# Window attention: inverse roots of two tiles at once on VectorE, and a new order of the rounds

## What is computed

```
for each of 6 blocks:                       # x is 16 x 256 x 128, 16 heads of 64
    q, k, v = split(x' @ Wqkv)              # x' : half of the channels shifted by one step
    q, k = l2norm(q) * qs, l2norm(k) * ks   # t / max(|t|, 1e-12)
    q, k = rotary(q, cos, sin, scale), rotary(k, cos, sin, 1 / scale)
    attn = softmax(mask(q @ k^T * 8))       # windows of 32 see themselves and the one before
    x = x + (attn @ v) @ Wo
    y = layernorm(shift(x)) * g + b
    x = x + (y1 * gelu(y2)) @ W2 + b2       # y1, y2 = split(y @ W1 + b1), 341 wide each
out = layernorm(x + x_before_the_stack)
```

## Time and profile before

| | us |
|---|---|
| median of 3 executions | 4148.47 (4144.48 to 4149.37) |
| profiled execution, its own time | 4148.09 |
| its span | 4146.3 |
| TensorE busy | 3788.5 (91% of the span) |
| GpSimd busy | 2942.9 (71%) |
| VectorE busy | 2900.7 (70%) |
| ScalarE busy | 2376.3 (57%) |
| mean granted TensorE clock | 0.961 of full speed |

### The profile page before, as it was taken

The page is one execution under the profiler, slowest core; times in us unless marked ns, Lnnn a source line. Parts: engine busy times, 40 slices in busy tenths (PEclk is TensorE's granted clock), DMA queues, the critical chain, the costliest instruction groups (busy, mean ns, idle before and its releaser), DMA issues.

```text
span 4146.3 us, 150150 instructions
## 1 busy us (share of the span) xinstructions
PE 3788.5 (91%) x64432; PEld 2730.8 (66%) x64432; DVE 2900.7 (70%) x5136; ACT 2376.3 (57%) x4221; POOL 2942.9 (71%) x4274
## 2 busy tenths in 40 slices
PE   6888899769999899998999989999899998999997
PEld 3444444357777677776777767777677776777774
DVE  3566655556777777777777777777777777777772
ACT  3322221146667667676666667776667766676662
POOL 0222222378888788887888878888788887888772
PEclk9999999879999999999999999999999999999998
DMA  1000000011111111111111111111111111111110
GB/s 67 3 6 6 6 3 3 16 47 39 38 36 41 46 45 41 38 39 41 48 42 37 40 39 49 42 38 40 40 44 46 39 37 44 42 48 41 40 36 25
DMA packets 96279, 147.03 MB, mean 35 GB/s; under 512 B 27264, under 2 KB 35840, under 8 KB 95488
## 3 DMA queue, kind: packets, MB, share of 16 engines
q1 hardware_dynamic: 95616, 137.42, 13.3%
HBM read 32.46 MB, written 4.19 MB: 9 GB/s over the span
## 4 chain that ended last, share of the span: by engine, by line
PE 80%; DVE 5%; POOL 5%; issue 4%; ACT 4%; DMA 1%; SPq 0%; POOLq 0%; ACTq 0%; DVEq 0%
PE bank L445 18%; PE bank L528 8%; PE bank L517 8%; PE bank L490 6%; PE bank L378 5%; PE bank L465 5%; PE bank L455 4%; PE bank L501 4%; PE bank L585 3%; PE bank L575 3%; PE bank L567 3%; PE bank L393 2%; PE bank L477 1%; POOL m L1341 1%; PE bank L420 1%
## 5 line engine op out<-in xcount | busy, mean ns | idle before, releaser
L445 PE MATMUL bank<-wqkv,xs 128*128 128x512 f32 x3456 | 1123.0, 441 | 18.2 <-DVE m L834 15.7
L1341 POOL TENSOR_TENSOR m<-m 128x512 f32<-128x512 f32 x768 | 969.2, 1283 | 67.8 <-DVE m L834 67.8
L445 PEld LDWEIGHTS bank<-wqkv,xs 128*128 128x128 f32 x3456 | 598.9, 194 | 161.7 <-issue 79.4
L832 DVE TENSOR_TENSOR m<-bank,tab 128x512 f32<-128x512 f32 x768 | 522.0, 680 | 216.3 <-ACT sq L1106 190.3
L1106 ACT ACTIVATE sq<-bank 128x512 f32<-128x512 f32 x768 | 456.4, 594 | 161.3 <-DVE ss L844 78.8
L834 DVE TENSOR_TENSOR m<-bank,tab 128x512 f32<-128x512 f32 x768 | 523.3, 681 | 18.5 <-POOL m L1341 18.5
L844 DVE TENSOR_REDUCE ss<-sq 128x8 f32<-128x512 f32 x768 | 503.4, 677 | 5.9 <-ACT sq L1106 5.1
L1349 POOL TENSOR_TENSOR S<-S,nw 128x1024 f32<-128x1024 f32 x192 | 365.3, 1902 | 193.2 <-DVE S L864 193.1
L517 PEld LDWEIGHTS bank<-P,big 64*64 64x64 f32 x24576 | 376.1, 135 | 97.7 <-issue 96.9
L1357 POOL TENSOR_TENSOR S<-S,rs 128x512 f32<-128x512 f32 x384 | 393.1, 1045 | 23.5 <-DVE rs L878 23.5
L1335 POOL TENSOR_TENSOR m<-m,nw 128x512 f32<-128x512 f32 x384 | 395.4, 1051 | 11.4
(11 more groups left out here) (202 smaller groups left out, 6600.7 us busy)
## 6 DMA issues: line engine op xcount, KB each, us to landing
big<-vst SPq DMA_DIRECT2D x1536, 64.0 KB, 2.0
stage<-in_wqkv SPq DMA_DIRECT2D x36, 256.0 KB, 3.0
tab<-in_tab SPq DMA_DIRECT2D x48, 128.0 KB, 2.3
big<-in_wa SPq DMA_DIRECT2D x1, 3460.0 KB, 12.5
wo<-in_wo SPq DMA_DIRECT2D x6, 512.0 KB, 3.7
big<-in_x SPq DMA_DIRECT2D x8, 256.0 KB, 3.2
keep<-Xr SPq DMA_DIRECT2D x8, 256.0 KB, 2.0
stage<-keep SPq DMA_DIRECT2D x8, 256.0 KB, 3.0
```

Source lines behind the costliest of these rows:

```text
L445: m = eng.matmul(pb[:, :], xt[a], wqkv[:, z, 512 * part:512 * part + 512], start=(n == 0), stop=(n == 2))
L832: eng.tensor_tensor(m1[:, part, :].rearrange("p (h d) -> p h d", d=DH), pv, ct.unsqueeze(1).to_broadcast([P, 8, DH]), ALU.mult)
L1341: eng.tensor_tensor(m1[:, part, :], m1[:, part, :], m2[:, part % 2, :], ALU.add).then_inc(s["g_add"], 1)
```

## The change

The chain moves from POOL to DVE. It is made once for two tiles, in the rounds with odd n, on 72 columns (32 of the even tile, 32 of the odd one, 8 for the layer norms), in nine instructions instead of twelve. The constant factor that two of the dropped instructions applied, `ROOT`, goes into the table of q and into `normed` and `ended`, which multiply by it in the same instruction as before.

Since the roots of an even tile are now ready a round later, all that follows k's scaling runs one tile later: `turn_k`, `mask`, `sim`, `largest`, `lessened`, `weighed` from n-1 to n-2, `exps`, `divide` to n-3, `probs`, `values` to n-4, `out_proj` to n-5; and the once-a-unit steps one unit later. A second buffer, `mk1`, holds parts 2 and 3 of odd tiles; `turned(g, part)` picks it. The loop bodies of PE, DVE, ACT and POOL are laid out anew. The core of the diff:

```diff
-STEPS, ROUNDS = 12, NG + 20
+STEPS, ROUNDS = 9, NG + 20
-ROOT = 1.0
+ROOT = 0.375 * FIRST
-    return STEPS * (g + 1 if g < NG else NG + (g - NG) // 4 + 1)
+    return STEPS * (g // 2 + 1 if g < NG else NG // 2 + (g - NG) // 4 + 1)
+        def turned(g, part):
+            return m1[:, part, :] if part < 2 or g % 2 == 0 else mk1[:, part - 2, :]
@@ vector @@
+            def chain(g):
+                if not 0 <= g < ROUNDS or g % 2 == 0 or g >= NG and g % 4 == 1:
+                    return
+                a = slice(0 if g < NG else 64, 72)
+                nm, y, t = (nw[:, g // 2 % 2, n, a] for n in range(3))
+                if g < NG:
+                    dv.wait_ge("v_ss", 4 * g + 4)
+                    dv.wait_ge("g_scl", 2 * (g - 3))
+                    dv.wait_ge("g_sub", g - 3)
...
+                dv.wait_ge("v_ch", n)
+                eng.tensor_scalar(nm, ss[:, g // 2 % 2, a], 3e38, 1e-24, ALU.min, ALU.max).then_inc(s["v_ch"], 1)
+                dv.wait_ge("v_ch", n + 1)
+                eng.tensor_scalar(y.bitcast(I32), nm.bitcast(I32), -0.5, MAGIC2, ALU.mult, ALU.add).then_inc(s["v_ch"], 1)
+                dv.wait_ge("v_ch", n + 2)
+                eng.tensor_tensor(t, y, y, ALU.mult).then_inc(s["v_ch"], 1)
+                dv.wait_ge("v_ch", n + 3)
+                eng.scalar_tensor_tensor(t, t, -1.0, nm, ALU.mult, ALU.mult).then_inc(s["v_ch"], 1)
...
-                eng.tensor_tensor(xn[:, :], lc, bank[RING["spread"]][:, :], ALU.mult).then_inc(s["v_xn"], 1)
+                eng.scalar_tensor_tensor(xn[:, :], lc, ROOT, bank[RING["spread"]][:, :], ALU.mult, ALU.mult).then_inc(s["v_xn"], 1)
...
-                largest(n - 1)
-                lessened(n - 1)
-                reduced(n, 2)
+                largest(n - 2)
+                if q4 == 3:
+                    norm_step(u - 2)
+                    end_step(u - 5)
                 reduced(n, 3)
...
+                lessened(n - 2)
+                if q4 == 0:
+                    low(u + 1)
+                chain(n)
+                residual(n - 4)
@@ gpsimd @@
-            def chain(g):
...
+                add(n - 1, 3)
+                scale(n - 2, 0)
+                scale(n - 2, 1)
                 add(n, 0)
                 add(n, 1)
...
+                weighed(n - 2)
```

More of the change, by code:

```diff
@@ L247, in _ @@
             eng.dma_start(w2, w2_d[0]).then_inc(s["d_down"], 16)
-            for n in range(NG + 28):
+            for n in range(NG + 32):
                 u, i = n // 4, n % 4
@@ L939, in end_step @@
                 dv.wait_ge("p_ev", k + 1)
-                dv.wait_ge("g_ch", rooted(4 * u + 16))
-                eng.tensor_scalar(ss[:, 0, 36:40], bank[RING["variance"]][:, 0:4], 1e-5, None, ALU.add).then_inc(s["v_e"], 1)
+                dv.wait_ge("v_ch", rooted(4 * u + 19))
+                eng.tensor_scalar(ss[:, 1, 68:72], bank[RING["variance"]][:, 0:4], 1e-5, None, ALU.add).then_inc(s["v_e"], 1)
             def ended(u):
@@ L977, in _ @@
                 weights(n, 3)
+                reduced(n, 2)
                 rotate(n, 3)
@@ L1228, in _ @@
                 q4, u = n % 4, n // 4
+                square(n, 0)
+                weights(n, 0)
+                probs(n - 4, 1)
+                square(n, 1)
+                weights(n, 1)
+                exps(n - 3)
+                if q4 == 1:
+                    gelu(u - 4, 0)
                 if q4 == 0:
                     high(u + 1)
-                probs(n - 3, 1)
-                square(n, 0)
-                weights(n, 0)
                 if q4 == 3:
-                    shifted(u - 1)
-                exps(n - 2)
+                    scaled(u - 3)
+                    shifted(u - 2)
                 if q4 == 1:
-                    gelu(u - 3, 0)
-                if q4 == 3:
-                    scaled(u - 2)
-                if q4 == 1:
-                    gelu(u - 3, 1)
-                square(n, 1)
-                weights(n, 1)
-                out_turned(n - 3, 0)
-                if q4 == 1:
-                    gelu(u - 3, 2)
+                    gelu(u - 4, 1)
                 v_out(n, 0)
                 square(n, 2)
-                turned_k(n - 1, 0)
-                turned_k(n - 1, 1)
+                turned_k(n - 2, 0)
+                turned_k(n - 2, 1)
                 square(n, 3)
-                turned_q(n, 0)
+                if q4 == 3:
+                    centred(u - 2)
+                    end_centred(u - 5)
+                out_turned(n - 4, 0)
+                if q4 == 1:
+                    gelu(u - 4, 2)
+                out_turned(n - 4, 1)
                 v_out(n, 1)
@@ L1258, in _ @@
                 weights(n, 5)
-                out_turned(n - 3, 1)
+                turned_q(n, 0)
                 turned_q(n, 1)
-                if q4 == 3:
-                    centred(u - 1)
-                    end_centred(u - 4)
-                probs(n - 2, 0)
+                probs(n - 3, 0)
         @block.gpsimd
```

223 lines of the change are left out of this document (95 added, 128 removed).

## The result

The changed kernel takes 4155.6 us (median of 19 runs, 4143.5 to 4162.7), the kernel before 4144.7 beside it (19 runs, 4130.1 to 4155.7). The ratio is 1.0026, interval 1.0016 to 1.0036: slower by 0.26%, some 11 us. The forecast was slower by 62 us.

A forecast was written before the change was run, and what follows sets the result against it. PE was taken to bound most of the run, POOL the first 13 tiles. Terms 79 - 28 + 9 - 10 + 21 gave +71 us on 4148.1; allowing for a pessimistic layout, the forecast was 4210 (+62), range 4105 to 4280.

The forecast's parts named there:

- The port: DVE chain steps with inputs in SBUF wait out the running POOL instruction; chain 5.0 us against 2.4 unhindered.
- The wait at `up`: In the q4 = 2 round PE waits at `up` for bank 3, freed by `residual`: 1.45 us a unit.
- The first 12 tiles: At the start, where POOL was the bound: 14.5 us a tile against 16.8, -28 us.
- Block-end stall: At the five block ends PE's stall becomes 13.9 us for 12.1, +9 us in all.
- tail: After the projections end, one unit more is left and one more attention round; +21 us.
- The base of 62.8: PE's own unit: 51.2 of plain rounds, 0.35 at `sim`, 10.8 feed-forward, 0.5 for `norm_step`; 62.8 us.
- The waits of 2.3: PE's losses to late DVE in a unit: 1.45 at `up`, 0.85 at bank 0 for `rotate`; 2.3 us.
- The irregular loss of 1.5: PE's irregular loss in each unit, 1.7 us in the kernel before, of which 1.5 was kept.
- C: Rival: the collision is there but PE loses only half as much; unit 65.4, total 4166 us; chance 0.15.
- B: Rival: chain runs unhindered at 2.4 us or DVE's lateness finds slack; unit 64.3, total 4103; chance 0.25 with neighbours.
- D: Rival: one more POOL instruction, `add(n, 2)`, queued at the chain; 1.3 us more each chain, total 4320; chance 0.08.
- The latency through `exps`: Rival: the extra round of latency uncovers `values` or `exps` waits; about 3 us in hand, no price, no chance given.

The follow-up runs named there:

- f1: Changed kernel with five-step-free full chain kept, GpSimd's `add(n, 3)` issued ahead of `weighed(n-2)` instead of behind it: 4094.1 us, ratio 0.9884 to the kernel before.
- e1: Changed kernel with the chain on VectorE placed ahead of `lessened` instead of behind it: 4134.4 us, ratio 0.9971 to the kernel before.
- b1: Kernel before with its GpSimd chain cut from twelve steps to six, second refinement left out: 4110.9 us, ratio 0.9922 to the kernel before.
- f4: Changed kernel with the last `add` ahead of `weighed` and `weighed` split into two halves: 4077.2 us, ratio 0.9842 to the kernel before.
- f7: Changed kernel with last `add` ahead of `weighed`, `weighed` in halves, and `wo` load issued one transfer group earlier: 4042.7 us, ratio 0.9750 to the kernel before.
- w1: Changed kernel with a new block's `wo` load issued one group of `vst` transfers earlier: 4124.8 us, ratio 0.9940 to the kernel before.
- f8: f7 with the chain also placed ahead of `lessened`: 4089.2 us, ratio 0.9853 to the kernel before.
- e4: Changed kernel with GpSimd's `add` of part 2 moved behind `weighed`: 4297.1 us, ratio 1.0371 to the kernel before.
- x1: Changed kernel with 64 one-column matmuls added once on PE ahead of `mask(8)`: 4179.6 us, ratio 1.0087 to the kernel before.
- x2: Changed kernel with 32 one-column matmuls added once on PE ahead of `mask(8)`: 4173.4 us, ratio 1.0065 to the kernel before.

## Why the prediction was right in sign, by luck, and wrong in size

**Right.** The port: 1.90 and 1.23 us for steps 2 and 3, chain 4.9 (5.0 forecast), and f1 and e1 take the waits away one by one. The rule as the prediction put it, for any DVE step with its inputs in SBUF, was too wide: `summed` (L913, 1.21) and `inverted` (L920, 0.24) read SBUF alone and take as long beside POOL as without it. The Trainium skill states this collision as an exclusive lock that one side holds for a whole instruction (SBUF — State Buffer, section SBUF: two separate sides); the traces agree, with L873 lasting the 1.90 us of `weighed`. The wait at `up`, 1.26 a unit (1.45 forecast). The first 12 tiles, -29.1 (-28), and b1 for their cause. Block-end stall 13.4 (13.9 for 12.1), tail +17.7 (+21). The last four units gained more than forecast, 67.3 each instead of 71.3.

**Wrong, the step that failed.** It is the pitch of a unit, 62.8 of PE's own work, 2.3 of waits and 1.5 of irregular loss, 66.6 in all. It measured 64.81. By its parts:

- The base of 62.8 is 62.1: that is the least unit of f4 and f7, whose rounds take 15.5, 16.1, 17.5 and 13.0, with hardly a wait for DVE but the 0.27 at `turn_q`. I had added 0.5 for `norm_step` (0.27 measured) and 0.35 for `sim` behind `turned_k` (PE idles 0.10 there); the rest of the 0.7 I can't name.
- The waits of 2.3 are 1.8: rounds of 15.5, 17.4, 17.5 and 13.5 in the least units of the changed kernel. The `up` round lost 1.3 (1.45), the `rotate` round 0.5 (0.85).
- The irregular loss of 1.5 is 0.9 (64.81 - 63.89).

Three terms that all leaned to one side, 0.7, 0.5 and 0.6 in a unit, make 1.8 x 40 = 72 us. The text said that the layout leans to the pessimistic side and took off 9.

**Wrong and hidden behind it.** "SP's queue and its later `wo`, `w1`, `w2` loads: nothing. The loads have whole rounds of cover." `wo` had none. It can't start before the last `out_proj` of the old block is over, and SP reaches it only behind `vst` transfers; what was left was 4.8 us before and 3.7 after. The 4.8 us were in the trace before, had I read the SP queue at a block end. It cost 31 us, so the rest of the forecast was off by 82 us, not by the 51 that the result shows. Without it the changed kernel is faster (w1, ratio 0.9940, interval 0.9923 to 0.9956), and the forecast would have been wrong in sign as well: the right sign was luck, two errors that partly cancelled.

**The rivals.** C, a unit of 65.4 and 4166, came nearest by its time. Its reason, half of the loss by waits, didn't hold: 1.8 of 2.3 are there. B asked for a chain of 2.4 us; e1 has that chain and takes 4134, and f8 comes below 4103 (4089) only with the earlier `wo`, which was worth 31 to 36. f4, with the chain at 3.6 and `weighed` kept early, takes 4077 without it. D's price of 1.3 for each chain was tried by e4: +142 us for 96 chains, 1.5 each, with its late `add` in it. The latency through `exps`, for which I had no price, didn't show in the changed kernel; in e1 and f8 ACT's longer wait speaks for it.

## What to carry to other kernels

A stall that is longer than another is not worth the difference: price it against the next limit, and try it a little shorter and a little longer (here 1.0 us less was worth 0.6, 1.0 more cost 1.5). When loops of several engines are laid out anew, look at each rare load (once a block) in the queue that issues it: what must end before it, what stands ahead of it, and how long from its issue to its first reader. Here small DVE steps on SBUF ran shortest where GpSimd had nothing ready to run (2.3 us for the chain), but ahead of the step that starts GpSimd's own long work that won less than it cost (f8 against f7, 46 us).

## What the runs showed of the hardware

- Of dependent DVE steps one gets through between two GpSimd instructions, whatever their size: f4 0.67 and 0.97, the changed kernel 1.90 and 1.23. A step with one input in SBUF waits as well (L873, 128x72), while one that reads PSUM (`rotate`, 0.68), a sum over SBUF (`summed`, 1.21 in both kernels) or a reciprocal of 128x16 in SBUF (0.24 in both) does not.
- TensorE stops 0.5 to 1.8 us inside runs of many small matmuls, at fixed places of its program (x1, x2, and 34 of 37 places shared by e1 and f8), each time until 1.12 to 1.61 us after a 16 KB piece of instructions had landed.
- A wait of 3.66 us on PE was followed by 6 us at a granted clock of 0.50: `out_proj` 3.76 us for 1.95. In the kernel before, without the wait, the clock was 1.00 there (2514 to 2518). A 512 KB load of `wo` needed about 3.7 us from its issue to the matmul (2502.43 to 2506.11).
